# Softmax attention in a fused four-stage kernel: the division by the row sums moves from the probabilities to the turned features, and the order of the transposes changes

## The reference, cut to what matters

```python
x = layernorm(x_in)
q, k, v = x @ Wq + bq, x @ Wk + bk, x @ Wv + bv       # each split into d = 4 groups of 64
scores = jnp.einsum('bdsh,bdth->bdst', q, k) / 2
weights = jax.nn.softmax(scores, axis=-1)             # exp(s - max) / sum over t
feats = jnp.einsum('bdst,bdth->bdsh', weights, v)
return feats @ Wo + bo                                # added to x_in
```

## Time and profile before

| what | value |
|---|---|
| median of 3 runs | 1712.46 us (1711.25 to 1715.58) |
| the profiled execution's own time | 1705.38 us |
| its span, first to last instruction | 1703.5 us |
| TensorE busy | 1492.6 us, 88% |
| VectorE busy | 1019.7 us, 60% |
| GpSimd busy | 875.0 us, 51% |
| ScalarE busy | 767.5 us, 45% |
| attention's loop, first scores to the last addition to x | 1353.30 to 1481.06 us |
| mean granted TensorE clock | 0.946 |

### The profile page before, as it was taken

One profiled execution on the slowest core, in us unless ns is written; L12 is line 12 of the kernel. 1 busy time (PEld: TensorE's weight loads), 2 busy tenths in 40 slices (PEclk: granted clock), 3 DMA queues, 4 the chain that ended last, 5 costly groups with the idle time before them and its releaser, 6 DMA issues. The chain is left out here.

```text
span 1703.5 us, 26260 instructions
## 1 busy us (share of the span) xinstructions
PE 1492.6 (88%) x9462; PEld 1077.1 (63%) x9462; DVE 1019.7 (60%) x2090; ACT 767.5 (45%) x1748; POOL 875.0 (51%) x1304
## 2 busy tenths in 40 slices
PE   2646999999999999999999999999769789689884
PEld 2324777787777777877777777777545445455553
DVE  2435777777767777677777776775530455451443
ACT  0322655656556556565565664654421245210111
POOL 0076676566665675666657666570100178315343
PEclk9677999999999999999999999999989899979997
DMA  8111111111111111101111111100052100012676
GB/s 203 44 31 35 36 26 36 34 38 35 22 39 32 35 35 35 38 23 32 41 29 38 35 28 36 32 20 13 7 228 96 31 1 1 30 51 78 132 146 144
DMA packets 126384, 86.25 MB, mean 51 GB/s; under 512 B 92146, under 2 KB 112454, under 8 KB 125488
## 3 DMA queue, kind: packets, MB, share of 16 engines
q1 hardware_dynamic: 120112, 76.04, 16.1%
q0 software_dynamic: 6144, 8.53, 3.0%
HBM read 61.45 MB, written 23.49 MB: 50 GB/s over the span
## 5 line engine op out<-in xcount | busy, mean ns | idle before, releaser
L580 PE MATMUL psum_banks<-main_hT,heads_w_in 128*128 128x512 f32 x512 | 248.1, 611 | 19.0 <-DVE heads_y L882 11.0
L882 DVE SCALAR_TENSOR_TENSOR heads_y<-psum_banks,gdn_conv_w,heads_y 128x1021 f32<-128x1021 f32 (+2 forms) x192 | 244.6, 1275 | 27.6 <-ACT heads_y L756 26.7
L1069 POOL TENSOR_TENSOR heads_XT<-heads_XT,heads_tmp 128x126 f32<-128x126 f32 (+22 forms) x496 | 207.4, 418 | 38.9
L1066 POOL TENSOR_TENSOR heads_tmp<-heads_XT,heads_A 128x126 f32<-128x126 f32 (+22 forms) x496 | 183.6, 370 | 38.9
L1405 POOL TENSOR_SCALAR attn_prob<-attn_prob,attn_rtotal 128x1024 f32<-128x1024 f32 x32 | 90.6, 2844 | 144.6 <-DVE attn_rtotal L1372 144.6
L580 PEld LDWEIGHTS psum_banks<-main_hT,heads_w_in 128*128 128x128 f32 x512 | 93.6, 195 | 94.3 <-issue 68.9
L667 PE MATMUL psum_banks<-heads_w_z,main_hT 128*128 128x256 f32 x512 | 126.8, 392 | 0.0
L756 ACT ACTIVATE heads_y<-psum_banks,gdn_conv_w 128x1024 f32<-128x1024 f32 x64 | 71.3, 1113 | 113.1 <-PE psum_banks L580 113.1
L693 PE MATMUL psum_banks<-heads_w_o,heads_ogT 128*128 128x256 f32 x512 | 119.2, 382 | 2.9 <-ACT heads_ogT L818 1.0
L778 ACT ACTIVATE heads_Dt<-heads_Dl,gdn_coef 128x128 f32<-128x128 f32 x224 | 77.3, 393 | 90.8 <-DVE heads_Dl L895 89.5
L1053 POOL TENSOR_TENSOR heads_Dm<-heads_Dm,main_upto 128x512 f32<-128x512 f32 x64 | 87.0, 1380 | 52.4 <-ACT heads_Dm L816 52.4
(11 more groups left out here) (243 smaller groups left out, 3416.5 us busy)
## 6 DMA issues: line engine op xcount, KB each, us to landing
main_w_gu<-in_w_gu SPq DMA_DIRECT2D x4, 2816.0 KB, 22.8
heads_w_in<-in_w_in SPq DMA_DIRECT2D x16, 512.0 KB, 3.5
heads_A<-kk_blocks SPq DMA_DIRECT2D x64, 128.0 KB
moe_wd<-in_w_down SPq DMA_DIRECT2D x32, 176.0 KB
expert_rows<-main_zeros SPq DMA_DIRECT2D x1, 4624.0 KB, 24.9
moe_be<-expert_rows SPq DMA_DIRECT2D x32, 144.5 KB, 3.2
heads_w_z<-in_w_z SPq DMA_DIRECT2D x16, 256.0 KB, 2.7
heads_w_o<-in_w_o SPq DMA_DIRECT2D x16, 256.0 KB, 2.6
```

Of the source, the lines that this page charges most:

```text
L580: ins = pe.matmul(out[:, half * 512:(half + 1) * 512], w_in[:, kd_, j * P:(j + 1) * P], hT[:, kd_, half * 512:(half + 1) * 512], start=kd_ ...
L882: dve.scalar_tensor_tensor(y[j][:, shift:T], src[:, 0:T - shift], conv_w[:, head, j, t:t + 1], y[j][:, shift:T], ALU.mult, ALU.add).then_i ...
L1066: pool.tensor_tensor(tmp[:, 0:n, 0:m], bc_last(XT[:, 0:n, j], m), bc_mid(A0[:, j, j + 1:BLK], n), ALU.mult).then_inc(solve_step.sem, 1)
L1069: pool.tensor_tensor(XT[:, 0:n, j + 1:BLK], XT[:, 0:n, j + 1:BLK], tmp[:, 0:n, 0:m], ALU.add).then_inc(solve_step.sem, 1)
```

## The change

GpSimd's multiply is gone. The probabilities are turned as they leave the exponential, undivided. Once per block, TensorE makes a tile of inverse sums in the layout of the turned features: the column of inverses of a head and step, repeated over 64 columns, is the stationary operand, the identity the moving one, so each of 64 output partitions holds the 128 inverses along its columns. Four such products fill columns 256 to 511 of the other `mix` bank. ScalarE copies the tile to SBUF (`rows_out`), and VectorE multiplies the features by it as they leave PSUM (`feats_out`, which was ScalarE's copy). The two heads' transposes stand apart in TensorE's order, with the part of the mixes between them, and they wait for the exponential alone. ScalarE now copies the first half and VectorE the second; ScalarE does head 0's copy ahead of the next exponentials. One reciprocal covers both heads of a step.

```diff
+        inverse = [a.sb(f"inverse{i}", [P, 2 * P]) for i in range(2)]
...
-                def transposes(p):
-                    for s in range(2):
-                        pe.wait_ge(s_norm, 2 * p + s + 1)
-                        for half in range(2):
+                def transposes(p, s):
+                    pe.wait_ge(s_exp, 2 * p + s + 1)
+                    for half in range(2):
...
                 def mixes(b, part):
                     if part == 0:
...
-                        if b >= 2:
-                            pe.wait_ge(s_ftw, b - 1)
+                        if b >= 1:
+                            pe.wait_ge(s_rowsw, b)
...
+                def inverse_rows(b):
+                    pe.wait_ge(s_rt, 2 * b + 2)
+                    if b >= 1:
+                        pe.wait_ge(s_ftw, b)
+                    for j in range(2):
+                        for s in range(2):
+                            n = 2 * (2 * b + j) + s
+                            ins = pe.matmul(mix[1 - b % 2][DH * s:DH * (s + 1), (2 + j) * P:(3 + j) * P],
+                                            rtotal[:, n:n + 1].to_broadcast([P, DH]), ident[:], start=True, stop=True)
+                    ins.then_inc(s_rows, 1)
...
                 for p in range(R):
                     if p + 1 < R:
                         scores(p + 1)
+                    transposes(p, 0)
                     if p >= 2:
                         mixes(p // 2 - 1, p % 2)
-                    transposes(p)
+                        if p % 2 == 0:
+                            inverse_rows(p // 2 - 1)
+                    transposes(p, 1)
...
                 for u in range(3):
                     outputs(u)
-                for part in range(2):
-                    mixes(BLOCKS - 1, part)
+                mixes(BLOCKS - 1, 0)
+                inverse_rows(BLOCKS - 1)
+                mixes(BLOCKS - 1, 1)
                 outputs(3)
...
             def _(act):
+                def rows_out(b):
+                    act.wait_ge(s_rows, b + 1)
+                    act.activation(inverse[b % 2][:], mix[1 - b % 2][:, 2 * P:4 * P], ACT.Copy).then_inc(s_rowsw, 1)
+
+                exponentials(0)
+                for p in range(R):
+                    first_half(p, 0)
+                    if p + 1 < R:
+                        exponentials(p + 1)
+                    first_half(p, 1)
+                    if p >= 2 and p % 2 == 0:
+                        rows_out(p // 2 - 1)
+                rows_out(BLOCKS - 1)
...
             def _(dve):
                 def feats_out(b):
                     f, t = pairs[2 * b]
+                    dve.wait_ge(s_mix, b + 1)
+                    dve.wait_ge(s_rowsw, b + 1)
+                    dve.tensor_tensor(featsT[:, f, t * P:(t + 2) * P], mix[b % 2][:, 0:2 * P], inverse[b % 2][:],
+                                      ALU.mult).then_inc(s_ftw, 1)
+
+                lows(0)
+                for p in range(R):
+                    if p + 1 < R:
+                        lows(p + 1)
+                    second_half(p, 0)
+                    dve.wait_ge(s_exp, 2 * p + 2)
+                    dve.reciprocal(rtotal[:, 2 * p:2 * p + 2], total[:, 2 * p:2 * p + 2]).then_inc(s_rt, 1)
+                    if p >= 2 and p % 2:
+                        feats_out(p // 2 - 1)
+                    second_half(p, 1)
                 feats_out(BLOCKS - 1)
...
-            @block.gpsimd
-            def _(pool):
-                for p in range(R):
-                    for s in range(2):
-                        n = 2 * p + s
-                        pool.wait_ge(s_rt, n + 1)
-                        pool.tensor_scalar(prob[p % 2][s][:], prob[p % 2][s][:], rtotal[:, n:n + 1], None, ALU.mult).then_inc(s_norm, 1)
```

More of the change, by code:

```diff
@@ L1270, in attention @@
         s_score, s_low, s_exp = a.sem("scores_ready"), a.sem("row_low_ready"), a.sem("probs_ready")
-        s_rt, s_norm, s_flip = a.sem("total_inverted"), a.sem("probs_divided"), a.sem("probs_flipped")
+        s_rt, s_flip = a.sem("total_inverted"), a.sem("probs_flipped")
+        s_rows, s_rowsw = a.sem("inverse_rows_ready"), a.sem("inverse_rows_written")
         s_pt, s_mix = [a.sem(f"probT_half{i}_written") for i in range(2)], a.sem("mixed")
@@ L1288, in scores @@
                                 ins.then_inc(s_score, 1)
-                def transposes(p):
-                    for s in range(2):
-                        pe.wait_ge(s_norm, 2 * p + s + 1)
-                        for half in range(2):
[L1294 to L1299, removed]
+                def transposes(p, s):
+                    pe.wait_ge(s_exp, 2 * p + s + 1)
+                    for half in range(2):
+                        if 2 * p + s >= 1:
+                            pe.wait_ge(s_pt[half], 2 * p + s)
+                        for j in range(4):
+                            k = half * 4 + j
+                            ins = pe.transpose(flip[half][:, j], prob[p % 2][s][:, k * P:(k + 1) * P], ident[:])
+                        ins.then_inc(s_flip, 1)
                 def mixes(b, part):
@@ L1341, in _, with exponentials @@
             def _(act):
+                def exponentials(p):
+                    for s in range(2):
+                        n = 2 * p + s
+                        act.wait_ge(s_low, n + 1)
+                        if p >= 2:
+                            act.wait_ge(s_flip, 4 * (p - 2) + 2 * s + 2)
+                        act.activation(prob[p % 2][s][:], score[s][:], ACT.Exp, bias=low[:, n:n + 1], scale=-1.0,
+                                       accum_out=total[:, n:n + 1]).then_inc(s_exp, 1)
@@ new lines, in first_half @@
+                def first_half(p, s):
+                    b = p // 2
+                    act.wait_ge(s_flip, 4 * p + 2 * s + 1)
+                    if p % 2 == 0 and s == 0 and b >= 2:
+                        act.wait_ge(s_mix, b - 1)
+                    act.activation(probT[b % 2][s][:, 0:4, (p % 2) * P:(p % 2 + 1) * P], flip[0][:], ACT.Copy).then_inc(s_pt[0], 1)
+                def rows_out(b):
+                    act.wait_ge(s_rows, b + 1)
+                    act.activation(inverse[b % 2][:], mix[1 - b % 2][:, 2 * P:4 * P], ACT.Copy).then_inc(s_rowsw, 1)
@@ new lines, in _, with lows, second_half @@
+                exponentials(0)
[7 more added lines that the diff above has]
+                rows_out(BLOCKS - 1)
+            @block.vector
+            def _(dve):
+                def lows(p):
+                    for s in range(2):
+                        n = 2 * p + s
+                        dve.wait_ge(s_score, n + 1)
+                        dve.tensor_reduce(low[:, n:n + 1], score[s][:], AX_X, ALU.min).then_inc(s_low, 1)
+                def second_half(p, s):
+                    b = p // 2
+                    dve.wait_ge(s_flip, 4 * p + 2 * s + 2)
+                    if p % 2 == 0 and s == 0 and b >= 2:
+                        dve.wait_ge(s_mix, b - 1)
+                    dve.tensor_copy(probT[b % 2][s][:, 4:8, (p % 2) * P:(p % 2 + 1) * P], flip[1][:]).then_inc(s_pt[1], 1)
@@ L1342, in feats_out @@
                 def feats_out(b):
                     f, t = pairs[2 * b]
[L1344 to L1348, removed]
-                        for s in range(2):
-                            act.wait_ge(s_low, 2 * p + s + 1)
-                            if p >= 2:
-                                act.wait_ge(s_flip, 4 * (p - 2) + 2 * s + 2)
-                            n = 2 * p + s
[L1354 to L1365, removed]
@@ L1366, in _ @@
-                feats_out(BLOCKS - 1)
[L1368 to L1392, removed]
```

## The result

| what | before | after |
|---|---|---|
| median of 4 runs, same chip | 1712.13 us (1711.25 to 1715.58) | 1698.74 us (1698.46 to 1699.05) |
| ratio | | 0.9918, 95% interval 0.9901 to 0.9935 |
| profiled execution's own time, span | 1705.38, 1703.5 | 1698.46, 1696.7 |
| GpSimd busy | 875.0 | 784.2 |
| attention's loop, first scores to last addition | 127.76 | 113.83 |

The change is 13.4 us faster (0.8%); the forecast was 9.0 and 1703.5, and 1698.74 lies 0.26 us under its range. The loop gave 13.9 us.

What follows compares the result with a forecast made beforehand. TensorE was taken to bound the steady loop, standing for copies. Gains of 5.7 us (steady steps), 3.0 (head) and 0.3 (tail) made 9.0, off the 1712.46 median: 1703.5 us, range 1699.0 to 1709.5.

Steps and rivals of the forecast that it cites:

- The mechanism: Steady loop: TensorE stands for copies of turned probabilities, not GpSimd's multiply; reordering the transposes removes 0.98 us of standing per step.
- Odd steps: Steady attention steps without the added tile: 5.88 us from scores to scores, instead of 6.74.
- The slacks: Spare time in a steady step: 0.07 us between ScalarE's early copy and first exponential, 0.23 before head 1's second half.
- B: ScalarE's early first-half copy holds up the exponentials, making the chain 6.2 us; total 1705.4; chance 0.12.
- D: TensorE's standing was not the limit; odd steps stay 6.74, even ones become 7.49; total 1713.8; chance 0.08.
- rival C: The half clock stays into the dense steps; three more such steps bring 1721.2 us; chance 0.07.
- The tile: Eight added small-product records on TensorE per block of two steps: 0.75 us, covered by nothing; even steps 6.63.
- The row of the upper bound: 14 weight loads with narrow moving tiles took 2.05 us, 0.146 each, so eight tile records cost 1.17 without overlap.
- The head: First three attention steps, second to fifth scores: 23.85 us becomes 20.8, a gain of 3.0, partly at low clock.
- The steps: Steady loop of eleven steps: six of 5.88 and five of 6.63, 68.43 us instead of 74.12, gain 5.7.
- The tail: End of attention: step 14 gains 0.1 and the stretch behind it 0.2, 0.3 us in all.
- The switch between kinds of tile: Added switch from scores to transposes on TensorE: scores still 1.92 us; upper price 0.12 more, a 6.00 step.

Runs made afterwards that it cites:

- the two experiments that take the change apart: Against the kernel before: new orders and copy split with GpSimd still multiplying, ratio 0.9932; division moved to the features with all old orders, ratio 1.0005.

## Why the prediction was wrong, point by point

**The mechanism held.** The wait that ends last in the steady loop was for the copies, not for GpSimd; the two experiments that take the change apart show it. Odd steps were forecast at 5.88 and came at 5.84 and 5.85. The slacks held (0.06 us before the first exponential, where 0.07 were forecast), so rivals B and D did not occur. The clock stayed at 1.00 from the third scores on: rival C did not occur.

**The sizes failed**, by 4.9 us in the loop (13.9 against 9.0), in three terms; the tile is the one that fails whatever the clock did.

*The tile.* The step "I take the weight loads of the mixes, 1.49 / 16 = 0.093 each" gave 0.75 us. A tile cost 0.44: its eight records and the switch behind them take 0.54, and the mixes ahead of it hand over 0.11 earlier, since the kind of tile stays the same (1.77 instead of 1.88). The tail's last tile, with mixes of the same kind behind it, shows the 0.44 bare (1462.98 to 1463.42). The row of the upper bound held moving tiles of up to 224 columns, not only narrow ones, so its 0.146 was no price of a weight load alone. The nearest bound was the low one, half the columns of a mix, 0.47; the weight loads hide beside the products:

```profile
1401.43 0.58 PEld L1325 LDWEIGHTS psum_banks<-main_ident,attn_rtotal 128*64 128x64 f32 x8
```

Five steady steps and two tiles in the tail make 7 x 0.31 = 2.2 us; the eighth tile is in the head.

*The head.* "Together 19.0 to 22.4; I take 20.8": it was 18.58, since from the third scores on the clock was full and the first two steps were 6.64 and 5.67, with 6.27 for the third; of the 0.4 under the low end 0.31 is the cheap tile. That is 2.2 us. The forecast put the clock's cost of the old kernel into the new one; the old head is the one that suffered, three falls in the profile it was read from. Another execution of the same kernel showed one fall and 2.6 us less, and against that head the gain is 2.65, near the 3.0 forecast. At full clock in both kernels it is 2.6. So about half of the 5.3 us gained in the head was a chance of the profiled execution and not of the change; how often the old head falls three times, two profiles don't tell.

*The steps.* 0.04 us less in each of twelve, 0.5 us: the switches out of the transposes took 0.10, not 0.12.

*The tail* was forecast to gain 0.3 and gained 1.0; the 0.7 are the two tiles counted above and a step.

**The switch between kinds of tile.** Scores followed by transposes took the same 1.92 as scores followed by mixes (1396.92 to 1398.84), so the upper bound, 0.12 more, fell. The Trainium skill, TensorEngine Tiling (Array Packing), Key Properties, says a change of mode drains the engine. The trace agrees, with a price for two of them: 0.11 us between mixes and a full-array product, about 0.10 between transposes and mixes. By these rows the added switch costs 16 x 0.10 = 1.6 us over the loop.

**The total.** The profiled execution of before lay 7 us under its median and that of after at its median. Taking the gain off the median was right; the spans alone would have shown half. That the loop's 13.9 and the medians' 13.4 are close is in part luck: 13.9 holds 2.6 us of the clock of one head, and the ratio's interval, 11 to 17 us, holds the 11.3 of equal clocks as well.

**The range.** It missed by 0.26 us. Its low end was the forecast less a full clock in the head (1.8), a cheap tile (2.2) and half a microsecond for the switch. All three happened, the tile with 0.3 more (8 x 0.31 = 2.5) and the head with 0.1: an end that is the sum of its best cases was the likely case here, since the tile's and the head's prices had been taken from the dear side of their bounds.

## What to carry to other kernels

Before crediting an engine's removal, ask which wait ends last: taking away GpSimd's 90.6 us gave 2.6 us of loop, most of it clock in one profile, and with the tile that replaces them it cost 0.8 in the steady steps; the orders and the place of the copies gave 8.5 there. Work added to a bound engine is priced by what it streams, with its loads beside it, and is free if it falls into a stand. And a short stage with stands at its start should be read from more than one execution, since the clock's falls differ from one to the next.

## What the runs showed of the hardware that was not expected

- Ten small products, 2.5 us of work in a stand of 3.65, kept the granted clock at 1.00 through the head in all three kernels that had them; without them it was 0.72 over the 6 us with the second scores, in the second profile of the changed kernel.
- Column-tiled products with 128 moving columns went at 0.44 us for eight records (0.54 with the switch to a transpose behind them), and a full-array transpose of 128 columns at 0.115 to 0.135.
- The stage behind attention, whose code is the same in all runs, took 222.4 to 242.4 us in the profiles, 235.1 or more on one chip and 227.7 or less on another, and the kernel before took 1707 us on the one with the shorter stage and 1719 to 1724 on the other, while the loop's steady steps agreed to 0.01 us. What in the chips makes the stage behind differ was not tried.
